# Transposing transfers of 1024 keys in place of 2048 in a full-size attention

## The chip, the core and the metric

The kernel runs on one core of one Trainium2 chip. The metric is the device time in microseconds (us) of one execution, as the median of three runs. A core has a matrix engine (PE), a vector engine (DVE), a scalar engine (ACT), a general engine (POOL), and a queue engine (SP) that here does nothing but wait on semaphores and issue DMAs. The sixteen DMA engines move the data of every issue.

## The reference, cut to what matters

The network has four layers on an input of 4 images, 128 channels and 64 x 64 positions. The first two are state-space layers, the third is a block-wise two-layer perceptron, and the fourth is an attention at three scales. The change is in the largest scale of the last layer:

```python
def _attention(x):                      # x: (4, 128, 64, 64), group-normalised
    B, C, H, W = x.shape
    xf = x.reshape(B, C, H * W)         # 4096 positions of 128 channels
    scores = jnp.einsum('bcn,bcm->bnm', xf, xf)
    attn = jax.nn.softmax(scores, axis=-1)
    out = jnp.einsum('bnm,bcm->bcn', attn, xf)
    return out.reshape(B, C, H, W)
out = jnp.zeros_like(x)
for scale in (4, 2, 1):
    block = _attention(_avg_pool(x, scale))
    out = out + jax.image.resize(block, (B, C, H, W), method='bilinear')
x = x + out                             # x before the normalisation
```

Scale 1 is the full-size attention: for each of 4 images a softmax over a 4096 x 4096 matrix of scores, which is never stored whole.

## The kernel before, in words

`program` runs the layers one after the other: two state-space layers (up to about 3440 us), the perceptron, then `attend`, which averages the input, runs the eight small attentions (`small_attentions`, 4 images of 256 positions and 4 of 1024) and last the full-size `attention`, from about 4184 us of the span to its end.

**Tiles.** A tile is 128 queries against all 4096 keys. An image has 32 tiles, the four images 128. Channels or queries lie on the 128 partitions. All products are made of two fp16 halves: `xh` is the high part of the normalised input and `xl` what is left over.

**One tile, engine by engine.**
- PE forms the scores in 8 banks of 512 keys, three products each (lines 1930 to 1932).
- DVE copies each bank to `s_sb` and takes its maximum (line 1999), then the row's maximum and the shift (lines 2006 and 2010). The shift needs all 8 banks.
- ACT then makes, in four pieces of 1024 keys (`EXPW`), the exponentials in fp16, `eh` (line 1975), and again in fp32, `s_sb` (line 1976).
- POOL forms for each piece the low part `el` = fp32 minus fp16 (line 1991).
- SP turns the exponentials so that keys lie on partitions: one transposing DMA from `eh` and one from `el` for each *part* of the keys (lines 2197 and 2199), into `et`. For the first tile of an image it also turns the values, `xl` and `xh`, into `vt` (lines 2205 and 2206), part by part, between the transfers of the exponentials.
- PE multiplies: 32 blocks of 128 keys, two products for each (lines 1946 and 1948), into `o_ps`; column 256 of `vt` is one, which gives the softmax's denominator. The result is scaled (lines 2016, 1982, 2022), turned by PE (line 1963) and added to `X` (line 2030).

**Parts.** `PARTS` is the number of parts into which the 4096 keys of a tile are cut for the transfers, `KEYS` = 4096 / `PARTS` their size, `PMT` = `KEYS` / 128 the blocks of 128 keys in one. Before, `PARTS` is 2, so a part has 2048 keys or 16 blocks, and is ready when two pieces of ACT and POOL are done. `eh` and `el` hold one tile, `et` two (its slot is chosen by the tile's parity and the part). Each part of `et` and of `vt` has a semaphore of its own.

**Order.** The order is written out by hand. In slot q of PE stand, bank by bank, the scores of tile q and then four key blocks of the values product of tile q-2. ACT and POOL work on tile q-1 in that slot. PE waits for a part of `et` at the first of its key blocks. ACT may write a part of `eh` again only when its transfer has landed; the same holds for POOL and `el`. SP issues strictly in its written order: for each part it waits until the values product two tiles back has freed the slot of `et` and `eh` is ready, issues `eh`, waits for `el`, issues `el`. Every fourth tile SP also loads two small tensors (`small2`, `small4`, line 2174, 102 KB and 36 KB) that DVE interpolates, and stores a finished group of four tiles (line 2182, 256 KB).

Of the kernel before, what the change touches and what calls it, by code (L numbers as in the profile page):

```python
# [1477 lines left out]
def attend(nc, sem, tag, X, C, scale_g, bias_g, final):  # L1478

    n2, n4 = PIX // 4, PIX // 16  # L1480
    size = {k: (N // k + 2) ** 2 for k in (2, 4)}

    kept = {k: nc.dram_tensor(f"{tag}_kept{k}", (P, B, size[k]), fp32, kind="Internal").ap() for k in (2, 4)}
    with Memory(nc, tag + "p") as pm:
        pooled = {2: pm.sb("pool2", [P, B, n2]), 4: pm.sb("pool4", [P, B, n4])}
        result = {k: pm.sb(f"out{k}", [P, B, size[k]]) for k in (2, 4)}
        average(nc, sem, tag, X, C, pooled, scale_g, bias_g)
        small_attentions(nc, sem, f"{tag}s", C, [(4, n4, pooled[4], result[4]), (2, n2, pooled[2], result[2])], kept)
    attention(nc, sem, f"{tag}s1", C, PIX, None, (X, scale_g, bias_g, kept, final), None)
# [318 lines left out]
def attention(nc, sem, tag, C, n, small, full, small_out):  # L1808
# [3 lines left out]
    NB = n // W  # L1812
    MT = n // P
    QT = n // P
    PARTS = min(2, NB)
    KEYS = n // PARTS
    PMT = KEYS // P
    EXPW = min(2 * BANK, KEYS)
# [5 lines left out]
    with Memory(nc, tag) as m:  # L1824
# [9 lines left out]
        s_sb = m.sb("s_sb", [P, 2, n])  # L1834
        eh = m.sb("eh", [P, PARTS, KEYS], fp16)
        el = m.sb("el", [P, PARTS, KEYS], fp16)
        et = m.sb("et", [P, 2, 2 * PARTS, PMT, P], fp16)
        tile_max = m.sb("tile_max", [P, 2, NB])
# [17 lines left out]
        s_xl = sem(f"{tag}_x_low")  # L1856
        s_vt = [sem(f"{tag}_values_turned{i}") for i in range(PARTS)]
        s_s = sem(f"{tag}_scores")
# [5 lines left out]
        s_el = sem(f"{tag}_exp_low")  # L1864
        s_eht = [sem(f"{tag}_exp_high_turned{i}") for i in range(2 * PARTS)]
        s_elt = [sem(f"{tag}_exp_low_turned{i}") for i in range(2 * PARTS)]
# [414 lines left out]
```

## Time and profile before

| | us |
|---|---|
| median of 3 runs (5743.13 to 5744.43) | 5743.19 |
| profiled execution, its own time | 5743.41 |
| profiled execution, span from first to last instruction | 5741.6 |
| full-size attention within the span | about 4184 to 5742 |

In the whole span PE is busy for 5020.8 us (87%), DVE for 4680.1 (82%), POOL for 4638.6 (81%) and ACT for 3523.7 (61%). Most of what DVE and POOL do belongs to the first two layers. So the shares of the whole say little on the last stage, and the page is to be read by its 40 slices: the last eleven are the full-size attention, where PE is 0.8 to 0.9 busy, DVE, ACT and POOL mostly 0.6 to 0.7, and the DMA engines 0.9 or more in all but the first. TensorE's granted clock is 0.9 or more of full speed there but for the first. Busy time of SP is not in that list: an issue of a DMA appears in the timeline as a row of engine SPq with its start and its length, and the view of one source line gives the shortest, middle and longest of them and the time from issue to landing.

### The profile page before, as it was taken

The numbers are of one execution on the slowest core, as the hardware profiler recorded it, in microseconds if no ns is written. First come the engines' busy times: TensorE is split into PE (matmuls) and PEld (weight loads), VectorE is DVE, ScalarE is ACT, GpSimd is POOL, SyncE is SP. The second block draws the span as 40 slices with busy tenths as digits, with TensorE's granted clock in tenths as the row PEclk, the third lists the DMA queues.
The fourth block names the chain that finished last, engine by engine and source line by source line (L and its number), as shares of the span: only waits on it lengthen the run. The fifth ranks groups of instructions, "written<-read, shape, count | busy, mean of one in ns | idle before, by whom it ended". The sixth has DMA issues, their size and how long they took to land. (4 is left out here: it accounts for less than half of the span.)

```text
span 5741.6 us, 69105 instructions
## 1 busy us (share of the span) xinstructions
PE 5020.8 (87%) x22870; PEld 2652.7 (46%) x22870; DVE 4680.1 (82%) x6531; ACT 3523.7 (61%) x4252; POOL 4638.6 (81%) x2131
## 2 busy tenths in 40 slices
PE   6899899998998998999999988883669989899898
PEld 3444444444444444444444444631446666666566
DVE  8999999999999999999999998203867767677665
ACT  4666676666766767666666663100557777777676
POOL 6999999999999999999999996101447767677676
PEclk9999999999999999999999999796889999999999
DMA  5555555555555555555555554294689999999999
GB/s 182 191 200 196 190 200 196 190 204 190 197 200 189 200 193 193 200 196 192 202 196 193 204 193 147 113 402 142 130 152 192 194 192 192 196 189 194 192 192 182
DMA packets 1407095, 1103.60 MB, mean 192 GB/s; under 512 B 1211642, under 2 KB 1221522, under 8 KB 1399316
## 3 DMA queue, kind: packets, MB, share of 16 engines
q1 hardware_dynamic: 1402264, 1097.96, 69.4%
q8 instruction: 183, 3.00, 0.2%
q10 hardware_dynamic: 4478, 1.25, 0.2%
q14 instruction: 170, 1.39, 0.1%
HBM read 780.67 MB, written 21.09 MB: 140 GB/s over the span
## 5 line engine op out<-in xcount | busy, mean ns | idle before, releaser
L853 POOL TENSOR_TENSOR mamba_state<-mamba_state,mamba_c_row 128x1024 f32<-128x1024 f32 x1024 | 2400.8, 2371 | 60.0 <-DVE mamba_state L818 60.0
L703 PE MATMUL mamba_y_ps<-mamba_state,ident 128*128 128x512 f32 x4096 | 1926.3, 598 | 144.1 <-POOL mamba_state L853 143.6
L818 DVE TENSOR_TENSOR_SCAN mamba_state<-mamba_decay,mamba_b_ps 128x1024 f32<-128x1024 f32 x768 | 1755.6, 2286 | 95.3 <-DVE mamba_b_ps L804 1.5
L1991 POOL TENSOR_TENSOR l3s_el<-l3s_s_sb,l3s_eh 128x1024 f16<-128x1024 f32 x512 | 1083.9, 2137 | 473.0 <-ACT l3s_s_sb L1976 444.4
L703 PEld LDWEIGHTS mamba_y_ps<-mamba_state,ident 128*128 128x128 f32 x4096 | 759.4, 189 | 894.3 <-issue 622.1
L1999 DVE TENSOR_SCALAR_CACHE_REDUCE l3s_s_sb<-l3s_s_ps 128x512 f32<-128x512 f32 x1024 | 705.4, 690 | 455.9 <-PE l3s_s_ps L1932 450.5
L804 DVE TENSOR_TENSOR mamba_b_ps<-mamba_dtu,mamba_b_ps 128x1024 f32<-128x1024 f32 x768 | 927.9, 1208 | 19.2 <-PE mamba_b_ps L691 18.5
L1946 PE MATMUL l3s_o_ps<-l3s_vt,l3s_et 128*128 128x257 f16 x4096 | 805.8, 275 | 130.7 <-DMA l3s_et<-l3s_el 90.2
L788 ACT ACTIVATE mamba_decay<-mamba_dt,mamba_A 128x1016 f32<-128x1016 f32 x768 | 846.5, 1134 | 12.7 <-DVE mamba_state L818 6.1
L1975 ACT ACTIVATE l3s_eh<-l3s_s_sb,l3s_shift 128x1024 f16<-128x1024 f32 x512 | 583.5, 1140 | 429.3 <-DVE l3s_shift L2010 406.9
L1948 PE MATMUL l3s_o_ps<-l3s_vt,l3s_et 128*128 128x129 f16 x4096 | 729.9, 221 | 0.0
L691 PE MATMUL mamba_b_ps<-mamba_bc,mamba_pick 128*128 128x512 f32 x1536 | 637.8, 496 | 100.8 <-DVE mamba_state L818 100.8
L847 POOL TENSOR_TENSOR mamba_b_row<-mamba_b_row,mamba_dtu 128x1024 f32<-128x1024 f32 x256 | 607.4, 2373 | 0.1
L818 DVE TENSOR_TENSOR_SCAN mamba_state<-mamba_b_ps,mamba_b_row 128x1024 f32<-128x1024 f32 x256 | 582.5, 2276 | 19.5 <-ACT mamba_b_ps L788 19.1
L1976 ACT ACTIVATE l3s_s_sb<-l3s_s_sb,l3s_shift 128x1024 f32<-128x1024 f32 x512 | 581.5, 1136 | 0.0
L1946 PEld LDWEIGHTS l3s_o_ps<-l3s_vt,l3s_et 128*128 128x128 f16 x4096 | 402.9, 98 | 343.1 <-issue 195.1
L691 PEld LDWEIGHTS mamba_b_ps<-mamba_bc,mamba_pick 128*128 128x128 f32 x1536 | 252.2, 189 | 517.7 <-DVE mamba_state L818 276.0
L1948 PEld LDWEIGHTS l3s_o_ps<-l3s_vt,l3s_et 128*128 128x128 f16 x4096 | 403.0, 98 | 102.7 <-issue 2.2
L1930 PE MATMUL l3s_s_ps<-l3s_xh 128*128 128x512 f16 x1024 | 391.2, 382 | 26.7 <-DVE l3s_xl L1901 25.9
L1931 PE MATMUL l3s_s_ps<-l3s_xl,l3s_xh 128*128 128x512 f16 x1024 | 391.0, 382 | 0.0
L1932 PE MATMUL l3s_s_ps<-l3s_xh,l3s_xl 128*128 128x512 f16 x1024 | 390.5, 381 | 0.0
L1512 POOL TENSOR_TENSOR l3v_pair<-X 128x2048 f32<-128x2048 f32 x4 | 14.4, 3604 | 380.6 <-SPq L1505 380.6
(330 smaller groups left out, 5902.3 us busy)
## 6 DMA issues: line engine op xcount, KB each, us to landing
mamba_c_row<-mamba_c_rows SPq DMA_DIRECT2D x1024, 512.0 KB, 3.7
mamba_b_row<-mamba_c_rows SPq DMA_DIRECT2D x256, 512.0 KB, 5.1
l_ring_a<-in_L_conv_W SPq DMA_DIRECT2D x28, 1024.0 KB, 10.9
l2b_ring_b<-in_L_conv_W SPq DMA_DIRECT2D x26, 1024.0 KB, 11.0
l_ring_a<-in_L_conv_W SPq DMA_DIRECT2D x14, 704.0 KB, 12.7
l2b_ring_b<-in_L_conv_W SPq DMA_DIRECT2D x13, 704.0 KB, 12.7
l_ring_a<-in_L_conv_W SPq DMA_DIRECT2D x14, 640.0 KB, 12.1
l2b_ring_b<-in_L_conv_W SPq DMA_DIRECT2D x13, 640.0 KB, 12.1
```

The lines of the kernel that those rows point to most:

```text
L691: last = nc.tensor.matmul(b_ps[s % PAIRS][:, half(h)], C["pick"][:, DVE_UNITS.index(s) * P:(DVE_UNITS.index(s) + 1) * P], bc[:, par, half( ...
L703: last = nc.tensor.matmul(y_ps[:, half(h)], C["ident"][:, :], state[:, s % STATES, half(h)], start=False, stop=(s == S - 1))
L788: nc.scalar.activation(seq(to), seq(dt[:, par, :]), ACT.Exp, scale=weights(c)["A"][:, s:s + 1]).then_inc(s_decay, 1)
L804: nc.vector.tensor_tensor(b_ps[s % PAIRS][:, :], dtu[:, par, :], b_ps[s % PAIRS][:, :], ALU.mult).then_inc(s_drive, 1)
L818: nc.vector.tensor_tensor_scan(state[:, s % STATES, :], by, add, 0.0, ALU.mult, ALU.add).then_inc(s_scan, 1)
L847: nc.gpsimd.tensor_tensor(row, row, dtu[:, par, :], ALU.mult).then_inc(s_bdrive, 1)
L853: nc.gpsimd.tensor_tensor(state[:, s % STATES, :], state[:, s % STATES, :], c_row[:, s % C_ROWS, :], ALU.mult).then_inc(s_hc, 1)
L1946: high = lambda stop: nc.tensor.matmul(o_ps[par][:, 0:2 * P + 1], et[:, 0, slot, j, :], vt[:, mt, 0:2 * P + 1], start=(mt == 0), stop=stop)
L1948: lows = lambda: nc.tensor.matmul(o_ps[par][:, P:2 * P + 1], et[:, 1, slot, j, :], vt[:, mt, P:2 * P + 1], start=False, stop=False)
L1975: nc.scalar.activation(eh[:, part, off:off + EXPW], src, ACT.Exp, bias=shift[:, par:par + 1]).then_inc(s_eh, 1)
L1991: nc.gpsimd.tensor_tensor(el[:, part, off:off + EXPW], s_sb[:, par, j * EXPW:(j + 1) * EXPW], eh[:, part, off:off + EXPW], ALU.subtract).t ...
L1999: nc.vector.tensor_scalar(s_sb[:, par, kb * W:(kb + 1) * W], s_ps[(par * NB + kb) % SLOTS][:, 0:W], 0.0, None, ALU.add, ALU.max, accum_out ...
```

## The change

The number of parts goes from 2 to 4 where the attention has at least four banks. `KEYS` becomes 1024, and `PMT` 8. The size of a piece of ACT and POOL is unchanged, since `EXPW` is the smaller of 1024 and `KEYS`. With `PARTS` change the shapes of `eh` and `el` (4 x 1024 in place of 2 x 2048), of `et` (8 slots of 8 blocks in place of 4 of 16), the number of semaphores of each kind, and the waits that stand at each part's start on PE, ACT, POOL and SP.

```diff
     NB = n // W
     MT = n // P
     QT = n // P
-    PARTS = min(2, NB)
+    PARTS = min(4, NB)
     KEYS = n // PARTS
     PMT = KEYS // P
     EXPW = min(2 * BANK, KEYS)
```

The instructions of PE, DVE, ACT and POOL are the same, in the same order. SP's list alone changes, from 1427 rows to 1955. At the first tile of an image, SP before (whole tile; `et<-eh` and `et<-el` are the exponentials, `vt` the values):

```order
L2197 DMA_TRANSPOSE l3s_et<-l3s_eh 128x16x128
L2199 DMA_TRANSPOSE l3s_et<-l3s_el 128x16x128
L2205 DMA_TRANSPOSE l3s_vt<-l3s_xl 128x16x128
L2206 DMA_TRANSPOSE l3s_vt<-l3s_xh 128x16x128
L2197 DMA_TRANSPOSE l3s_et<-l3s_eh 128x16x128
L2199 DMA_TRANSPOSE l3s_et<-l3s_el 128x16x128
L2205 DMA_TRANSPOSE l3s_vt<-l3s_xl 128x16x128
L2206 DMA_TRANSPOSE l3s_vt<-l3s_xh 128x16x128
```

And SP now, the first two parts of that tile:

```order
L2197 DMA_TRANSPOSE l3s_et<-l3s_eh 128x8x128
L2199 DMA_TRANSPOSE l3s_et<-l3s_el 128x8x128
L2205 DMA_TRANSPOSE l3s_vt<-l3s_xl 128x8x128
L2206 DMA_TRANSPOSE l3s_vt<-l3s_xh 128x8x128
L2197 DMA_TRANSPOSE l3s_et<-l3s_eh 128x8x128
L2199 DMA_TRANSPOSE l3s_et<-l3s_el 128x8x128
L2205 DMA_TRANSPOSE l3s_vt<-l3s_xl 128x8x128
L2206 DMA_TRANSPOSE l3s_vt<-l3s_xh 128x8x128
```

Eight issues that turned 16 blocks each have become sixteen that turn 8 each (two more parts follow these). At the other 31 tiles of an image, here the second with the small loads ahead of it, SP before:

```order
L2174 DMA l3s_small<-l_kept 128x204
L2174 DMA l3s_small<-l_kept 128x72
L2197 DMA_TRANSPOSE l3s_et<-l3s_eh 128x16x128
L2199 DMA_TRANSPOSE l3s_et<-l3s_el 128x16x128
L2197 DMA_TRANSPOSE l3s_et<-l3s_eh 128x16x128
L2199 DMA_TRANSPOSE l3s_et<-l3s_el 128x16x128
```

and now:

```order
L2174 DMA l3s_small<-l_kept 128x204
L2174 DMA l3s_small<-l_kept 128x72
L2197 DMA_TRANSPOSE l3s_et<-l3s_eh 128x8x128
L2199 DMA_TRANSPOSE l3s_et<-l3s_el 128x8x128
L2197 DMA_TRANSPOSE l3s_et<-l3s_eh 128x8x128
L2199 DMA_TRANSPOSE l3s_et<-l3s_el 128x8x128
L2197 DMA_TRANSPOSE l3s_et<-l3s_eh 128x8x128
L2199 DMA_TRANSPOSE l3s_et<-l3s_el 128x8x128
L2197 DMA_TRANSPOSE l3s_et<-l3s_eh 128x8x128
L2199 DMA_TRANSPOSE l3s_et<-l3s_el 128x8x128
```

Four issues a tile have become eight of half the size. The loads and stores stand where they stood, between the same tiles.

## Rows read from the trace of the kernel before

**Rows 1.** Busy time by engine: a stretch of 24 tiles, then the whole full-size attention.

```profile
core 0: us, PE busy (x) PEld busy (x) DVE busy (x) ACT busy (x) POOL busy (x), PEclk, DMA share, GB/s
4670.00:4955.00 285.00, 268.71 (x2212) 181.40 (x2210) 205.37 (x692) 216.35 (x225) 211.14 (x100) 1.00 1.12 193
4184.00:5742.00 1558.00, 1401.01 (x11392) 942.87 (x11392) 1061.63 (x3585) 1113.98 (x1153) 1083.94 (x512) 0.98 1.08 187
```

**Rows 2.** The line of the shift, 4670:4955 and 5420:5700 (ns least/median/most, first and last start).

```profile
L2010 DVE TENSOR_SCALAR l3s_shift<-l3s_row_max x24: 153/154/155, 4680.5 to 4944.5; 128x1 f32<-128x1 f32 x24
...
L2010 DVE TENSOR_SCALAR l3s_shift<-l3s_row_max x24: 153/154/155, 5427.0 to 5694.7; 128x1 f32<-128x1 f32 x24
```

**Rows 3.** Waits, 4184:5742 (us in total, times, longest us).

```profile
PE l3s_o_ps L1946 <- DMA l3s_et<-l3s_el: 90.2, 121, 3.2
PE l3s_o_ps L1946 <- DMA l3s_vt<-l3s_xh: 27.2, 6, 11.5
SPq L2199 <- POOL l3s_el L1991: 241.6, 124, 3.8
```

**Rows 4.** The chain of waits, 4680:4706 (start us, us, what).

```profile
4680.49 0.16 DVE l3s_shift L2010
...
4685.34 1.98 POOL l3s_el L1991
...
4687.51 4.96 DMA l3s_et<-l3s_el
...
4692.60 0.27 PE l3s_o_ps L1946
...
4703.05 0.17 DVE l3s_shift L2010
```

**Rows 5.** Timeline of POOL from 4681.

```profile
4683.00 2.15 POOL L1991 TENSOR_TENSOR l3s_el<-l3s_s_sb,l3s_eh 128x1024 f16<-128x1024 f32 x1 [2.80 <-ACT l3s_s_sb L1976]
```

**Rows 6.** Timeline of SP, first tile of the second image.

```profile
4599.88 2.23 SPq L2205 DMA_TRANSPOSE l3s_vt<-l3s_xl  x1
4602.16 2.45 SPq L2206 DMA_TRANSPOSE l3s_vt<-l3s_xh  x1
4604.70 2.21 SPq L2197 DMA_TRANSPOSE l3s_et<-l3s_eh  x1
...
4612.01 2.40 SPq L2206 DMA_TRANSPOSE l3s_vt<-l3s_xh  x1
```

**Rows 7.** Issue lines of the full-size attention (ns least/median/most, landings of exponentials).

```profile
L2197 SPq DMA_TRANSPOSE l3s_et<-l3s_eh x256: 1532/2460/3876, 4217.3 to 5727.7; - x128
DMA to landing us min/median/max: 4.3/4.9/7.1
...
L2174 SPq DMA_DIRECT2D l3s_small<-l_kept x64: 319/447/1178, 4184.0 to 5651.3; - x64
...
L2182 SPq DMA_DIRECT2D out<-X x32: 332/683/1042, 4317.1 to 5739.2; - x32
```

**Rows 8.** Issue lines of the small attentions: 8 blocks, 4 blocks, 16 blocks.

```profile
L1754 SPq DMA_TRANSPOSE l3s_vt<-l3s_xh x3: 1302/1302/1302, 4097.6 to 4149.9; - x3
DMA to landing us min/median/max: 2.8/2.8/3.4
...
L1758 SPq DMA_TRANSPOSE l3s_etl<-l3s_ehl x8: 1188/1206/1210, 4048.8 to 4065.7; - x8
...
L1758 SPq DMA_TRANSPOSE l3s_etl<-l3s_ehl x24: 1473/1609/2395, 4094.7 to 4169.4; - x24
```

**Rows 9.** Timeline of SP in the small attentions, two transfers of 8 blocks.

```profile
4067.04 1.26 SPq L1753 DMA_TRANSPOSE l3s_vt<-l3s_xl  x1
4068.35 1.30 SPq L1754 DMA_TRANSPOSE l3s_vt<-l3s_xh  x1
```

**Rows 10.** Timeline at the stage's start: ACT and POOL.

```profile
4214.05 1.15 ACT L1975 ACTIVATE l3s_eh<-l3s_s_sb,l3s_shift 128x1024 f16<-128x1024 f32 x1 [28.78 <-DVE l3s_shift L2010]
...
4216.38 8.40 POOL L1991 TENSOR_TENSOR l3s_el<-l3s_s_sb,l3s_eh 128x1024 f16<-128x1024 f32 x4 [44.46 <-ACT l3s_s_sb L1976]
```

**Rows 11.** Timeline at the end: SP's last transfers, PE's last part.

```profile
5727.74 1.78 SPq L2197 DMA_TRANSPOSE l3s_et<-l3s_eh  x1
5729.58 2.73 SPq L2199 DMA_TRANSPOSE l3s_et<-l3s_el  x1
...
5734.65 0.27 PE L1946 MATMUL l3s_o_ps<-l3s_vt,l3s_et 128*128 128x257 f16 x1 [0.23 <-DMA l3s_et<-l3s_el]
...
5737.20 0.27 PE L1946 MATMUL l3s_o_ps<-l3s_vt,l3s_et 128*128 128x257 f16 x1
```

## The prediction

> **What bounds the kernel now.** Only the last 1558 us of the span are touched, so I read the stretches of busy time first. In 24 undisturbed tiles PE is busy for 268.7 of 285 us, POOL for 211, ACT for 216, and the DMA engines are shown busier than they can be, 1.12 of sixteen [rows 1]. Two things are near full: PE and the DMA queue. The starts of the shift, one a tile, give the pace: (4944.5 - 4680.5) / 23 = 11.48 us, and later (5694.7 - 5427.0) / 23 = 11.64 us [rows 2]. At a busy share of 0.943, PE needs 11.48 x 0.943 = 10.82 us of it. So about 0.7 us a tile is stall.
>
> The waits name it: PE waits 121 times for a landing of `el`, 90 us in all, which is once a tile [rows 3]. The chain of waits shows how the wait closes on itself. From the shift at 4680.49 to the first values product of that tile at 4692.60 are 12.1 us: ACT's exponentials, POOL's second piece of `el`, which ends the part at 4687.51, and a transfer of 5 us. From there it is 10.45 us to the shift two tiles on, at 4703.05 [rows 4]. That is 22.56 us for two tiles, 11.3 a tile. The first part is what is late, since it needs two of POOL's pieces and a full transfer.
>
> Third, SP. An issue of 16 blocks takes 2.46 us in the middle here, 1.53 at best [rows 7], while the same size takes 1.61 in the small attentions [rows 8]. Where nothing is waited for, six issues stand one behind the other, the sixth 4612.01 - 4599.88 = 12.13 us after the first, so 2.43 us each [rows 6]: that is the pace at which the queue takes 16 blocks, and SP is held to it. Four a tile make 9.7 us. Yet SP also stood waiting for `el` 124 times, 242 us in all [rows 3]; part of these waits lies beside issues that were still held by the queue, so their sum is not idle time.
>
> **The change, part by part.**
>
> *The loop's latency.* The first part is ready after one piece of POOL: at 4683.00 + 2.15 = 4685.15 [rows 5], 2.4 us sooner. An 8-block transfer lands 2.8 us after issue [rows 8], against 5. Shift to values becomes 4.66 + 2.8 + 0.1 = 7.6 us, and the loop (7.6 + 10.45) / 2 = 9.0 us a tile. That is under PE's 10.82: the wait that bounds the kernel now is gone. Later parts have more slack yet, since PE reaches each of them 2.7 us after the last and POOL needs 2.1 us for one.
>
> *What is late next: SP.* It issues eight transposing transfers a tile. What one costs depends on its floor, since half of 2.43 is 1.22 us and no longer holds SP. Three kinds of row bound the floor: 4 blocks take 1.21 us and 16 blocks 1.61 [rows 8], 8 blocks 1.26 and 1.30 [rows 9], and three more 1.30 [rows 8]. The 1.26 had an empty queue before it, the 1.30 another 8-block transfer. The exponentials lie together in memory, the values do not, which could make them either cheaper or the same. I take 1.28 for exponentials and 1.31 for values; the lower end is 1.21, the upper 1.34, on the straight line from 4 to 16 blocks. From one issue's end to the next start go 0.05 us inside a pair (4068.35 - 4067.04 - 1.26, rows 9), and 0.09 where two waits lie between (4604.70 - 4602.16 - 2.45, rows 6).
>
> The list from the first `el` to the last, in order:
> - 1022 exponentials x 1.28 = 1308.2 us
> - 32 value transfers x 1.31 = 41.9 us
> - 62 small loads x 0.45 and 30 stores x 0.68 = 48.3 us, medians of [rows 7]
> - gaps: 559 x 0.05 + 587 x 0.09 = 80.8 us
>
> Sum 1479.2 us, or about 11.2 a regular tile. That is more than PE's 10.82 and the loop's 9.0, so SP is the bound, and its waits are covered by its own backlog. I add 10 us for the starts of images and for transfers that stall now and then (the longest landing is 7.1 us against 4.9, rows 7).
>
> *The start.* ACT's first piece ends at 4215.2 and POOL's at 4216.38 + 2.1 = 4218.5 [rows 10], where the list begins. Last `el` issued: 4218.5 + 1479.2 + 10 = 5707.7, against 5729.6 now [rows 11].
>
> *The end.* Now 12.0 us follow it: 5.0 for the landing, 2.8 for sixteen key blocks (5734.65 to 5737.5), 4.2 for the rest [rows 11]. With half the size they are 2.8 + 1.4 + 4.2 = 8.4. The span ends at 5716.1. The profiled time lies 1.8 us over its span, and the median 0.2 under the profiled time: 5718.
>
> *At nothing.* PE, ACT and POOL get more waits, at each part's start. ACT and POOL have over 2.5 us a tile to spare [rows 1], PE 0.4 under the new pace. `eh` and `el` may now be written a quarter at a time, no later than before. The value transfers' bytes do not change: PE waits for the first quarter only, but SP must still issue all of it, so the 27 us that PE now waits for values [rows 3] are not given back but turned into SP's time, which stands in the sum.
>
> *A rule against the change.* These rows show small transfers going out every 1.31 us with 2.8 us to landing, so landings overlap. The Trainium skill, "DMA: Bandwidth & Descriptors", section "Rules for kernel authors", says to join many small transfers into a large one; its section on the anatomy of one DMA, measured on the software path, puts a fixed 2.0 us on each, beside the bytes. By that rule, if the fixed parts came one after another, eight transfers would cost 16 us a tile for the fixed part alone, and the stage would be over 500 us slower. The trace disagrees for this path: the fixed part overlaps with other transfers, and what does not overlap is SP's issue.
>
> **Rivals.**
>
> *Issue costs more than it did beside light traffic (slower).* At SP's two lines, L2197 and L2199, 8 blocks cost 1.34 us or more: 1022 x 0.06 = 61 us over my sum, 5779. The point from which it decides is 1.30 to 1.31, where the gain of 25 us is used up. For it: every 8-block row but one is at 1.30 to 1.32, and 16 blocks go from 1.61 to 2.46 in this stage. Against it: 2.46 is the queue's pace, not SP's, and an idle start in this stage took 1.53, less than 1.61.
>
> *SP is not the bound (faster still).* If an issue takes 1.21 as with 4 blocks, the list shrinks by 72 us to 1408, 10.7 a tile, and PE's 10.82 decides. Against 11.56, the mean of the two paces of now, that is 0.74 x 124 tiles = 92 us, with the ends about 5650. Between, at 1.25, lies 5687. For it: 4 and 8 blocks differ little. Against it: no 8-block row is under 1.26.
>
> *Nothing to measure.* The first wait is gone but the DMA engines stay the limit: they show 1.12 now and have the same bytes to move. If their pace with stalls is 11.4 a tile, only the ends' 3.6 us remain, 5740. For it: the DMA share. Against it: SP waits for POOL once a tile, in which the queue can drain; the pace of 2.43 for 16 blocks gives only 9.7 a tile and some 0.6 for loads and stores.
>
> **Numbers.** SP-bound at about 1.28: 0.40. SP not the bound: 0.14. Nothing to measure: 0.17. Issue dearer: 0.29. About 0.2%, 11.5 us, is what a measurement of this kernel tells from no change. Faster than 5731.7 needs an issue under 1.293: nearly all of the first case and the second, 0.52. Within: 0.18. Slower: 0.30. The range goes from 5680 (1.24) to 5785 (a little over 1.34); the likeliest case alone spans 5700 to 5735.
>
> **What would show it.** Right: issues at L2197 and L2199 in the middle near 1.28 us, SPq rows standing one behind the other with 0.05 to 0.09 between them, landings near 3 us, PE's waits for `et` spread over the four parts of a tile, a shift every 11.2 to 11.3 us, hardly a wait of SP for POOL. Wrong: a middle issue over 1.30 (slower), or SP rows with holes between them and a shift every 10.8 us (faster), or issues of 8 blocks above 1.4 held by a queue with no gap between transfers (the DMA engines are the limit). PE's, DVE's, ACT's and POOL's durations should not move.

## The result and the profile after

| | us |
|---|---|
| before, median of 4 runs beside it | 5743.81 |
| after, median of 4 runs (5809.54 to 5815.41) | 5812.21 |
| ratio after / before, 95% interval | 1.0118 (1.0100 to 1.0136) |
| profiled execution after, its own time and span | 5815.41, 5813.6 |

The change makes the kernel 68 us slower. In the profile after, the busy time by engine (stretch and whole stage, against [rows 1]) is:

```profile
core 0: us, PE busy (x) PEld busy (x) DVE busy (x) ACT busy (x) POOL busy (x), PEclk, DMA share, GB/s
4670.00:4955.00 285.00, 259.17 (x2126) 173.62 (x2125) 202.28 (x676) 211.29 (x216) 203.19 (x96) 1.00 1.10 185
4184.00:5813.00 1629.00, 1420.27 (x11392) 943.77 (x11392) 1065.46 (x3585) 1131.12 (x1153) 1088.59 (x512) 0.97 1.06 180
```

All engines have become idler, and the DMA engines move 185 GB/s where they moved 193. Nothing that this view lists is fuller, and SP is not in it. The shift's line gives the pace in the same two stretches:

```profile
L2010 DVE TENSOR_SCALAR l3s_shift<-l3s_row_max x23: 153/154/155, 4681.3 to 4944.0; 128x1 f32<-128x1 f32 x23
...
L2010 DVE TENSOR_SCALAR l3s_shift<-l3s_row_max x22: 153/153/155, 5435.9 to 5691.6; 128x1 f32<-128x1 f32 x22
```

That is 262.7 / 22 = 11.94 us and 255.7 / 21 = 12.18 us a tile, against 11.48 and 11.64 [rows 2]. SP's timeline shows what fills that time (start, us):

```profile
4691.89 1.31 SPq L2197 DMA_TRANSPOSE l3s_et<-l3s_eh  x1
4693.25 1.33 SPq L2199 DMA_TRANSPOSE l3s_et<-l3s_el  x1
4694.67 1.30 SPq L2197 DMA_TRANSPOSE l3s_et<-l3s_eh  x1
4696.01 1.33 SPq L2199 DMA_TRANSPOSE l3s_et<-l3s_el  x1
4697.46 1.28 SPq L2197 DMA_TRANSPOSE l3s_et<-l3s_eh  x1
4698.78 1.34 SPq L2199 DMA_TRANSPOSE l3s_et<-l3s_el  x1
...
4720.24 1.42 SPq L2197 DMA_TRANSPOSE l3s_et<-l3s_eh  x1
4721.70 1.79 SPq L2199 DMA_TRANSPOSE l3s_et<-l3s_el  x1
```

One issue stands behind the other, in the middle with 0.05 us between `eh` and `el` and 0.09 after `el`, and no hole. SP is at its bound. Most issues take 1.28 to 1.34 us, but now and then one takes 1.8 or more. Over the whole stage (least/middle/most in ns):

```profile
L2197 SPq DMA_TRANSPOSE l3s_et<-l3s_eh x512: 1231/1292/2528, 4219.0 to 5801.6; - x171
...
DMA to landing us min/median/max: 3.1/3.4/5.3
...
L2199 SPq DMA_TRANSPOSE l3s_et<-l3s_el x512: 1231/1336/2721, 4222.3 to 5803.0; - x171
```

The waits of PE and ACT (total, times, longest) show where this surfaces, against [rows 3]:

```profile
PE l3s_o_ps L1946 <- DMA l3s_et<-l3s_el: 141.5, 128, 2.4
ACT l3s_eh L1975 <- DMA l3s_et<-l3s_eh: 130.8, 144, 4.5
```

The second of these stood at 22.1 us before:

```profile
ACT l3s_eh L1975 <- DMA l3s_et<-l3s_eh: 22.1, 10, 6.3
```

PE waits for `el` about as often as before, half as long again in total. ACT now waits for its own buffer: SP is so late that the quarter is still in transfer when the next tile wants to write it.

One line of SP's own waits is not to be taken at its word:

```profile
SPq L2199 <- POOL l3s_el L1991: 233.9, 262, 2.1
```

It says that SP waits for POOL as long as before. But POOL's piece had ended before the row of the issue began in all 512 cases, 4.6 us before it in the middle, and between the rows there is no such time.

I summed all rows of SP from the first `el` to the last transfer, in both profiles. The transposing transfers are those of `et` and `vt`; a hole is a stretch over 0.15 us between two of them that holds neither a load nor a store.

| us | before | after | predicted list |
|---|---|---|---|
| exponentials: number, mean issue | 512, 2.53 | 1024, 1.37 | 1.28 |
| all transposing issues | 1331 | 1447 | 1350 |
| loads and stores | 56 | 48 | 48 |
| between the issues | 125 | 87 | 81, and 10 for stalls |
| first `el` to last transfer's end | 1512 | 1582 | 1490 |

Before, some 49 us of the 125 are the gaps that every issue has, and about 76 us are true holes. After, holes of some 3 us are left: the list has grown until it fills the stage.

### The profile page after: what moved, and what is told of

It reads as the page before. It is cut to its first block and busy times, and to the rows that moved or that the text cites. A ratio compares the mean times of both kernels' runs of the same rounds, so it can differ in the third digit from the quotient of the medians.

```text
span 5813.6 us, 70417 instructions
## 1 busy us (share of the span) xinstructions
PE 5042.2 (87%) x22870; PEld 2655.3 (46%) x22870; DVE 4687.1 (81%) x6531; ACT 3540.6 (61%) x4252; POOL 4642.5 (80%) x2131
```

## The experiments

Ratios are against runs of the kernel before on the same chip, with their 95% interval.

**Issues without finer parts.** Two parts as before, each transfer issued in two halves.

```diff
-sp.dma_start_transpose(et[:, 0, slot, :, :], eh[:, part, :]).then_inc(s_eht[slot], 16)
+for at in range(EXB * FIRST[part], EXB * last, step):      # step = 8 blocks
+    sp.dma_start_transpose(et[:, 0, par, at:at + step, :],
+                           eh[:, at * P:(at + step) * P]).then_inc(s_eht[slot], 16)
```

> Two parts as before, with before's waits and semaphores at each part, but every transposing transfer (exponentials and values) issued as two of 8 blocks one behind the other. Theory S (the stage is bound by the time that SP needs to issue, by the number of issues): the list of SP is as long as in the changed kernel, 1056 transfers at a mean of 1.37 us, so the time is that of the changed kernel, 5812, or up to 15 us more since the first part is late again. Rival G (what costs is the finer parts themselves: more waits on PE, ACT and POOL, buffers written again in quarters): parts are as before, so 5744. Rival Q (the same bytes in smaller transfers move more slowly through the DMA engines): 5812, as S; the third run parts them.

Measured 5823.5, ratio 1.0138 (1.0121 to 1.0155). Parts, buffers and waits of before, and yet the time of the changed kernel. The finer parts (G) are not what costs; the number or the size of the transfers is. The 11 us over the changed kernel lie within the 15 that were allowed for the late first part. Its issues look like those after:

```profile
L2216 SPq DMA_TRANSPOSE l3s_et<-l3s_el x512: 1231/1343/2832, 4212.4 to 5797.3; - x171
```

**Finer parts without more issues.** Four parts, but `eh` and `el` of a part are neighbours in one buffer `ehl` and go out together.

```diff
 wait(sp, s_eh, ready)
-sp.dma_start_transpose(et[:, 0, slot, :, :], eh[:, part, :]).then_inc(s_eht[slot], 16)
 wait(sp, s_el, ready)
-sp.dma_start_transpose(et[:, 1, slot, :, :], el[:, part, :]).then_inc(s_elt[slot], 16)
+sp.dma_start_transpose(et[:, par, 2 * EXB * FIRST[part]:2 * EXB * last, :],
+                       ehl[:, 2 * EXPW * FIRST[part]:2 * EXPW * last]).then_inc(s_eht[slot], 16)
```

> Four parts, but the fp16 exponentials and their low part of one part lie side by side and go out in one transfer of 16 blocks once both are ready: four issues a tile as before, values in 8 transfers of 8 blocks an image. S: SP issues 4 x 2.43 us a tile at most and is no longer the bound; the first part needs one piece of POOL, 4.7 us, and a landing of 5, so the loop is (9.7 + 10.45) / 2 = 10.1 us a tile and PE with 10.8 to 11.0 decides: 5665 to 5700. G: parts are as fine as in the changed kernel, 5800 or more. Q: transfers are as large as before, 5744 or a little less.

Measured 5716.95, ratio 0.9948 (0.9932 to 0.9965): faster than both kernels. With the first, this closes the case on G from both sides. The gain of 29 us is less than the 44 to 79 that S had: SP's rows show issues of 16 blocks, held by the queue, one behind the other (x5 are five merged):

```profile
L2212 SPq DMA_TRANSPOSE l3s_et<-l3s_ehl x512: 1513/2414/4235, 4219.9 to 5707.8; - x171
...
4703.91 13.06 SPq L2212 DMA_TRANSPOSE l3s_et<-l3s_ehl  x5
```

Its list is 1352 us of transposing issues, 56 of loads and stores and 83 between, 1490 in all. I had expected PE to decide. It does not; the queue's pace does.

**The same transfers, fewer other issues on SP.** The changed kernel with `load_small` and `store` called by ACT.

```diff
+            if exps and at % 4 == 1 and at + 4 <= B * QT:
+                load_small(act, at // 4 + 1)
...
+                if j == 3 and exps and at % 4 == 3 and at > 3:
+                    store(act, at // 4 - 1)
```

> The changed kernel with the 64 small loads and 32 stores issued by ACT in place of SP; the transfers are the same and as many. S: SP is rid of 94 issues within its list, 32 + 16 us and 94 gaps of 0.09, together 57 us: 5755, if ACT's 48 us hide in its idle time. Q: bytes and sizes are the same, so 5812. G: 5812.

Measured 5783.56, ratio 1.0068 (1.0051 to 1.0085), 29 us less than the changed kernel. Same bytes and sizes, other time: that is SP's time and not the transfers' alone. But only half of the 57 us came back. The transposing issues rose from 1447 to 1473 us, 120 of them over 1.5 us in place of 91. Of the 120, 96 lie beside an instruction fetch (next experiment) and 24 do not. All 24 stand within 0.5 us of a load or store under way, as only 247 of all 1056 issues do. Loads and stores now move while SP issues, and by these rows they hold it. The Trainium skill, "DMA: Bandwidth & Descriptors", "Rules for kernel authors", says that spreading DMAs over issuing engines saves only sequencer time, since they share the DMA engines; this run agrees, with 29 us saved of 57.

**Is PE in it, and what holds the long issues?** The second product of each key block left out.

```diff
-                if mt == MT - 1:
-                    lows()
-                    last = high(True)
-                else:
-                    high(False)
-                    last = lows()
+                last = high(mt == MT - 1)
```

> The changed kernel without the second product of each key block (the low part of the exponentials is still formed and turned, but not used): 4096 of 128x129 and their weight loads are gone from PE. S: PE is not the bound. Of 1024 issues 89 took over 1.5 us, 59 us more than the others in all, and 88 of these lay beside one of the 92 fetches of 16 KB on the instruction queue; if those fetches are PE's, a third of them goes with a third of its instructions, 33 x 0.65 = 21 us: 5790. If PE bounded the stage: 32 x 54 ns x 128 = 220 us less, 5590. If held issues have another cause: 5812.

Measured 5787.4, ratio 1.0070 (1.0053 to 1.0086): 25 us less, where S had 21 and a bound on PE 220. In both profiles I compared the times of SP's issues over 1.5 us with those of the packets on queue q8, which the page of the profile calls instruction: of 91 such issues after, 90 had one that began during the issue or up to 2.5 us before it; without the low product 59 of 59. Of all 1056 issues after, 204 had one. The queue's own rows for the stage, after and then in this run:

```profile
q8 instruction: 92, 1.51, 0.4%
```

```profile
q8 instruction: 60, 0.98, 0.2%
```

A third of PE's instructions gone, a third of the fetches gone, a third of the long issues gone (91 to 59, and the excess over the middle of those of the exponentials from 58 to 38 us). The fetches are PE's: from one to the next lie on average 257 matmuls and weight loads in the profile after, and 256 in this run. By their share, 0.4% of the DMA engines, the fetches are nothing; what they cost is that the transfers pause. In the profile after, 177 packets of transfers start in an average quarter of a microsecond. Between 0.5 and 1.75 us behind the start of a fetch, averaged over the 92, it is 8 to 38. Then the pace is back. So the trace shows fetch, pause and held issue together; no run changed the fetches alone, and what in a fetch makes the others pause is open.

**Between two and four.** Parts of 1024, 1024 and 2048 keys (`SIZES = (1, 1, 2)`).

> Three parts of 1024, 1024 and 2048 keys: six transfers a tile, four of 8 blocks and two of 16. S, with the means measured so far: 512 x 1.37 + 256 x 2.45 + 40 for values + 48 for loads and stores + gaps 62 = 1478 us of SP, 104 less than the 1582 of the changed kernel. But the run with joined transfers stood at 1489 with its 16-block transfers one behind the other, which looks like the queue's own limit. So 5705 to 5720, a gain of 25 to 40 over before. If the loop through the first part, not SP, were still what counts, all runs with a first part of 1024 keys would be alike, 5812.

Measured 5772.31, ratio 1.0046 (1.0029 to 1.0062): between, but 52 us over the upper end of the expectation. SP is full again: 1400 us of transposing issues, 59 of loads and stores, 74 between, 1532 in all, 54 more than in my list. The list had 2.45 us for 16 blocks and 1.37 for 8; here the means are 2.48 and 1.42, which makes 31 of the 54 with the values, and the rest are loads and stores (11) and gaps (12). So 16-block issues cost here about what they cost where all have 16 blocks (2.53 before), and 8-block issues no less than where all have 8. A mixture is no better than its parts. The 16-block issues vary, from 1.7 to over 3 us; these are two long ones:

```profile
4691.90 1.29 SPq L2212 DMA_TRANSPOSE l3s_et<-l3s_eh  x1
4693.24 1.34 SPq L2216 DMA_TRANSPOSE l3s_et<-l3s_el  x1
4694.67 3.15 SPq L2212 DMA_TRANSPOSE l3s_et<-l3s_eh  x1
4697.86 3.00 SPq L2216 DMA_TRANSPOSE l3s_et<-l3s_el  x1
```

**The loop of waits.** Parts of 1024 and 3072 keys (`SIZES = (1, 3)`).

> Two parts of 1024 and 3072 keys: four transfers a tile as before, two of 8 blocks and two of 24, the first part as early as in the changed kernel. If the number of issues and the first part were all (S alone): 1426 us of SP, so the queue's limit, 5715. Theory L, the loop of waits by part: the second part is ready when POOL ends, 11.1 us after the shift, and lands some 6.3 later; PE needs it after a quarter of a tile, 7.8 us before the shift two tiles on; (17.4 + 7.8) / 2 = 12.6 us a tile against 11.56: 5875.

Measured 5980.01, ratio 1.0403 (1.0386 to 1.0420). The fewest issues with an early first part, and the slowest of the short lists: here 356 us lie between SP's rows, against 87 after, and the loop through the late part decides, as L said. The pace is (4942.4 - 4685.4) / 19 = 13.5 us a tile, not 12.6:

```profile
L2022 DVE TENSOR_SCALAR l3s_shift<-l3s_row_max x20: 153/153/155, 4685.4 to 4942.4; 128x1 f32<-128x1 f32 x20
...
L2216 SPq DMA_TRANSPOSE l3s_et<-l3s_el x256: 1231/2922/4747, 4220.7 to 5968.9; - x128
DMA to landing us min/median/max: 3.0/5.4/7.6
```

The landing was not what I had too small: 24 blocks of `el` land in 5.7 us in the middle, against my 6.3. The estimate left out a wait of POOL for its own buffer:

```profile
POOL l3s_el L2003 <- DMA l3s_et<-l3s_el: 126.8, 62, 6.1
```

In a third of the tiles (43 of 124) POOL is done 13.1 us after the shift in the middle and not 11.2, since `el` of the tile before is still in transfer. With it, and 0.4 us from POOL's end to the issue, the loop is (13.1 + 0.4 + 5.7 + 7.8) / 2 = 13.5. Long and short distances between shifts, 16 and 11 us, mostly alternate.

**The dose.** Four parts, sixteen issues of 4 blocks a tile.

> Four parts, each transfer issued as two of 4 blocks: sixteen issues a tile. The suspected cost doubled. S: 4-block issues took 1.21 us beside light traffic, so 2112 x 1.23 + 48 + gaps 150 = 2796 us of SP against 1582: 7025. If the cost went by bytes or by parts: 5812.

Measured 7137.7, in one run. The number of issues doubled again and 1325 us more, for the same bytes. The issue of half the size is hardly cheaper:

```profile
L2212 SPq DMA_TRANSPOSE l3s_et<-l3s_eh x1024: 1188/1260/2617, 4219.3 to 7123.8; - x171
```

The DMA engines are at half their share meanwhile, 0.54 against 1.10, so it is not they that hold these issues (Q):

```profile
4670.00:4955.00 285.00, 182.17 (x1135) 108.66 (x1135) 103.84 (x354) 116.31 (x117) 110.56 (x52) 0.85 0.54 101
```

The forecast of 7025 fell short by 113 us, since it had 1.23 us an issue and the mean is 1.29. There are 92 issues over 1.5 us, and again 92 fetches; each such issue has one beside it:

```profile
q8 instruction: 92, 1.51, 0.2%
```

Twice as many issues over nearly twice the time, and not one more is held: the holds go with PE's instructions, 256 from one fetch to the next here too.

From 4 blocks to 8 the middle issue goes from 1.26 to 1.29 (`eh`) and from 1.27 to 1.34 (`el`). So some 1.2 us of it belong to the issue and not to what it moves. But the length of a row alone misleads, for it and the gap ahead of it make up for each other. In this run a row after a gap of 0.10 us takes 1.21 in the middle, one after 0.04 takes 1.27. From start to start it is the same 1.31 us in both cases:

```profile
4803.44 2.52 SPq L2212 DMA_TRANSPOSE l3s_et<-l3s_eh  x2
4806.00 2.58 SPq L2216 DMA_TRANSPOSE l3s_et<-l3s_el  x2
4808.68 2.52 SPq L2212 DMA_TRANSPOSE l3s_et<-l3s_eh  x2
```

These four issues take (4808.68 - 4803.44) / 4 = 1.31 us each. With 8 blocks, in the profile after, it is 1.385 in the middle, be it 0.09 and 1.29 or 0.05 and 1.34. Before, the small attentions had the same: 4 blocks take (4061.85 - 4059.24) / 2 = 1.31, and two issues of 8 blocks 1.38 and 1.41.

```profile
4059.24 2.51 SPq L1758 DMA_TRANSPOSE l3s_etl<-l3s_ehl  x2
4061.85 1.20 SPq L1753 DMA_TRANSPOSE l3s_vt<-l3s_xl  x1
...
4120.70 1.33 SPq L1753 DMA_TRANSPOSE l3s_vt<-l3s_xl  x1
4122.08 1.30 SPq L1754 DMA_TRANSPOSE l3s_vt<-l3s_xh  x1
4123.49 1.67 SPq L1758 DMA_TRANSPOSE l3s_etl<-l3s_ehl  x1
```

So apart from the held ones an issue is no dearer in this stage than in the small attentions.

**The best version.** Joined transfers, loads and stores on ACT; then again, beside the kernel before with only its loads and stores on ACT.

> The joined transfers of four parts, with the small loads and the stores issued by ACT. If SP's issuing bounds the joined kernel: 57 us less, 5660. If the DMA queue's pace does (16 blocks in 2.4 us, whoever issues the rest): the loads and stores still move, 5705 to 5717.

> The kernel before (two parts), with the small loads and the stores issued by ACT. In the trace of before SP's issues of 16 blocks are held by the queue, and SP stood idle for some 77 us of the stage. If 16-block issues are held by the queue's pace (S with the queue): the 57 us of SP's issues mostly turn into longer holds, and the loop of waits still counts: 5720 to 5740. If SP's own time bounded before too: 57 us less, 5687.

> The best kernel so far once more, with more rounds: joined transfers of four parts, loads and stores on ACT. From the run before 5702, a ratio near 0.9925; against the run beside it (two parts, loads and stores on ACT) it should be 20 to 35 us faster, which is the gain of the joined quarters alone.

Measured 5701.96 (ratio 0.9925, 0.9908 to 0.9941) and, again, 5702.71 (0.9925, 0.9911 to 0.9938). It is the fastest version, 43 us under before, 3 us under the lower end that the queue's pace was expected to give, and 37 us faster than two parts with loads and stores on ACT, where 20 to 35 were expected. Those measured 5739.43, 0.9990 (0.9981 to 0.9999): some 6 us, with an interval from 1 to 11. There 16-block issues are held anyway:

```profile
L2217 SPq DMA_TRANSPOSE l3s_et<-l3s_el x256: 1526/2622/4182, 4225.9 to 5724.2; - x128
```

For `el` the middle one has gone from 2.54 us to 2.62. SP's freed time became longer holds. The two edits are worth some 6 and 29 us alone and 43 together.

## Why the prediction was wrong

*What bounds before.* Right in its parts: a loop of waits through the first part, and a queue nearly full. The joined run, which shortens the loop and leaves the issues, gains 29 us; the run with 3072 keys in the last part shows that the loop decides when it is long. Too strong was that the loop alone was the bound: before, SP's list with its held issues already filled 1512 - 76 of 1512 us, so with issues of that length at most some 76 us were to be had. The 242 us of SP's waits for `el` [rows 3] were no such reserve, as the prediction suspected.

*The loop goes, SP is next.* Right, and the forecast that SP's rows would stand one behind the other with 0.05 and 0.09 us between them holds in the middle; in all the gaps took 87 us and not 81. PE waits at all four parts of a tile, as forecast (65, 34, 38 and 16 times at the first block of each). The shift comes every 11.9 to 12.2 us, not 11.2 to 11.3, and 8 blocks land in 3.4 us, not 3.

*The size of the list: this step failed.* "I take 1.28 for exponentials" and "I add 10 us" for transfers that stall. Measured are 1.344 us for `eh` and 1.399 for `el` as means, 1404 us in all in place of 1024 x 1.28 = 1311, 94 us more. It has two parts. The middle issue is 1.29 and 1.34, which makes 35 us. All eight 8-block rows in the trace of before but one took 1.30 to 1.33, and from start to start they took 1.37 to 1.41 but for that one; the prediction took a value between the short row and the others and put the mean gap beside it, 1.28 + 0.07 = 1.35 where 1.385 was measured. And the mean is 0.05 and 0.06 over the middle, 59 us, because about 90 issues are held for 0.65 us each. Before, such holds were in sight as landings of up to 7.1 us [rows 7], but they fell on issues that waited for the queue anyway. I priced them at 10 us, as before shows them, and not as a full SP pays for them: each in full. The time, too, is 94 us over the forecast, but that the two numbers agree is chance: the 10 us for stalls come off, 7 for gaps, 6 for the start and the end and 2 for the values are added, and the median is 3 us under the profiled execution.

*The upper bound.* 1.34 was the end of the range for the typical issue, and it was a good one. It was no bound on the mean of 1.37. The range up to 5785 left the held issues out.

*The rivals.* The dearer issue is what happened, at the lines that it names; its price of 5779 was 33 us short, since it had no held issues either. Its reason fits in part: beside the light traffic of the small attentions an issue of 8 blocks took as long from start to start, so what this stage adds are the holds. The point from which it decides, 1.30 to 1.31, agrees with what was measured as a mean: 68 us spread over 1024 issues are 0.067, and 1.372 - 0.067 = 1.305. That the change could not gain while the DMA engines stay full (*nothing to measure*) is not what limited it: their pace fell from 193 to 185 GB/s.

*The end and the start.* The end took 10.6 us in place of 8.4. The list began at 4222.3 in place of 4218.5, since the stages ahead, which the change does not touch, ended later in this execution.

## What to carry to other kernels

Cutting a transfer in two doubles what the issuing engine pays, and that engine is in no list of busy time: look for its rows in the timeline, and add them up before and after. If one issue of the larger size is already held by the queue, half the size pays only down to the floor of an issue, here 1.39 us from start to start against 2.6 for twice the data. Take that distance from start to start, and not the length of a row and a gap from different places. To get a finer first part without more issues, join streams that become ready together. And an engine that is made the bound pays every stall in full that it hid before: take the mean of its instructions, not the middle.

## What the runs showed of the hardware

- Transposing transfers that stand one behind the other on SP take, from start to start and in the middle, 1.31 us for 4 blocks of 128 x 128 fp16 (DMA share 0.54) and 1.385 for 8 (1.10). For 16 the issue alone is held to 2.4 to 2.6 (1.11 to 1.15).
- PE's instructions are fetched in pieces of 16 KB, one for every 256 or so matmuls and weight loads (256 to 257 in four profiles). Between 0.5 and 1.75 us behind the start of a fetch hardly any other packet starts, 8 to 38 in a quarter of a microsecond against 177 on average. The 92 fetches have 0.4% of the DMA engines' time and go with 58 us of held issues once SP is the bound.
- 96 plain loads and stores moved to ACT's queue save SP some 57 us of its own time; 29, 15 (the joined kernel, 5717 to 5702) or 6 us of it come back in the end, the less the more SP is held by the queue.
